# A mixture-of-experts layer on one core: in each slot the down projection of three chunks back is issued ahead of the gate and up projections

## The chip, the core and the metric

The kernel runs on one core of one Trainium2 chip. The metric is the device time of one execution in microseconds (us). The engines are PE (TensorE, the matmuls; PEld is its weight load), DVE (VectorE), ACT (ScalarE), POOL (GpSimd) and SP (SyncE, which here issues most of the DMAs). Each works through its own instructions in program order; semaphores tie them together.

## The reference

`x` is 2 x 2048 tokens of width 128. The layer is a macaron: half a feed-forward, attention with 16 heads of width 8, and half a feed-forward again with the same weights.

```python
x = x + 0.5 * ffn(layernorm(x))
x = x + attn(layernorm(x))
x = x + 0.5 * ffn(layernorm(x))
...
# ffn: 8 routed experts (top 2 of a softmax), I = 176, and one shared expert with a sigmoid gate
g = einsum('th,ehi->eti', x, w_gate)
u = einsum('th,ehi->eti', x, w_up)
eo = einsum('eti,eih->eth', silu(g) * u, w_down)
out = einsum('te,eth->th', combine, eo) + sg * (silu(x @ sw_gate) * (x @ sw_up) @ sw_down)
```

## The kernel before

All 8 experts and the shared one are computed for every token. Their 9 x 176 = 1584 hidden rows are put one after the other and cut into CH = 13 chunks of 128 (the last, the tail, has 48). Tokens come in NB = 8 blocks of 512. A step of the work is one chunk of one block, so a feed-forward has N = 104 chunks. The function `expert_phase` runs it; it is called twice, as "e1" before the attention and as "e3" after it.

For chunk n the work passes through the engines like this:

1. PE, gate (L598): three matmuls of 512 columns (high and low parts of weights and tokens) into one of two PSUM banks.
2. PE, up (L606): three matmuls into another bank. The tail chunk has no such matmuls, because its 48 up rows ride in the unused rows of its gate matmuls.
3. ACT, silu of the gate (L644).
4. POOL, times the expert's weight for each token, `cw` (L674).
5. DVE, `multiply` (L688): times up, back into PSUM.
6. ACT, `high` (L651): the product rounded to fp32r, into one of three buffers (`q_head` by name, whose room it borrows).
7. DVE, `low` (L694): what the rounding left over. It raises the semaphore `hidden_ready`.
8. PE, down (L616): three matmuls that add the chunk to the block's sum in bank Y.

PE's order is written out by hand in slots: slot s issues gate and up of chunk s and, DOWN_AFTER = 3 slots behind, the down projection of chunk s-3. DVE's order in slot s is `multiply(s)`, then `low(s-1)`; ACT's is silu of s, then `high(s-1)`. At the end of a block ACT copies bank Y out (L664), PE transposes it (L634) and DVE adds it to x (L707).

What PE waits for: gate of chunk n for the silu of chunk n-2 (for the multiply, where n-2 is a tail); up of chunk n for `low` of chunk n-4 in e1 (UPS = 4 banks), and of chunk n-3 in e3 (UPS = 3); down of chunk n for `low` of chunk n.

In e3 the object `beside` (class `Late`) puts work of the second half of the batch at the end of the slots: on PE the spreading of softmax sums (L1383), the output projection (L1398), transposes and router scores; on DVE additions and statistics (L1405, L1408), normalisation (L1443), and the router's many small steps (L1519 to L1549, slots 37 to 43).

Of the kernel before, what the change touches and what calls it, by code (L numbers as in the profile page):

```python
# [542 lines left out]
def expert_phase(nc, sem, tag, ps, x, xnT, wgate, wup, wdown, comb_rows, comb_stored, ident, room, stats=None,  # L543
# [19 lines left out]
    CW, HIDDENS, DOWN_AFTER = 8, BUFS, 3  # L563
# [12 lines left out]
    with ExitStack() as tmp:  # L576
# [11 lines left out]
        N = NB * CH  # L588

        @block.tensor  # L590
        def _(pe):
            def up(n):
                blk, c = divmod(n, CH)
                cols, tokens = slice(c * P, (c + 1) * P), slice(blk * BLK, (blk + 1) * BLK)
                if n >= 2:
                    pe.wait_ge(product if (n - 2) % CH == CH - 1 else silued, n - 1)
                for m, (wp, xp) in enumerate(PASSES):
                    last = pe.matmul(ps[:, GATE + n % 2, :], wgate[wp][:, cols], xnT[xp][:, tokens],  # L598
                                     start=(m == 0), stop=(m == len(PASSES) - 1))
                last.then_inc(gated, 1)  # L600
                if c == CH - 1:
                    return
                if n >= UPS:
                    pe.wait_ge(hidden_ready, n - UPS + 1)
                for m, (wp, xp) in enumerate(PASSES):
                    last = pe.matmul(ps[:, UP + n % UPS, :], wup[wp][:, cols], xnT[xp][:, tokens],  # L606
                                     start=(m == 0), stop=(m == len(PASSES) - 1))
                last.then_inc(upped, 1)

            def down(n):  # L610
                blk, c = divmod(n, CH)
                pe.wait_ge(hidden_ready, n + 1)
                if c == 0:
                    pe.wait_ge(summed_kept, blk + PRIME)
                for m, (wp, hp) in enumerate(PASSES):
                    last = pe.matmul(ps[:, Y, :], wdown[wp][0:rows[c], c, :], hidden[hp][n % HIDDENS][0:rows[c], :],  # L616
                                     start=(c == 0 and m == 0), stop=(c == CH - 1 and m == len(PASSES) - 1))
                last.then_inc(downed, 1)

            for s in range(N + DOWN_AFTER + 1):  # L620
                if s < N:
                    up(s)
                if DOWN_AFTER <= s < N + DOWN_AFTER:
                    down(s - DOWN_AFTER)
                if beside is not None:
                    beside.beside_pe(pe, s, SIDE)
                blk, c = divmod(s - DOWN_AFTER - 1, CH)
                if c == CH - 1 and blk >= 0:
                    pe.wait_ge(summed_kept, blk + 1 + PRIME)
                    pe.wait_ge(added, blk + PRIME)  # L630
                    if beside is not None:
                        beside.leave_bank(pe, blk)
                    for j in range(TPB):
                        tr = pe.transpose(ps[:, YT, j * P:(j + 1) * P], yT[:, j * P:(j + 1) * P], ident[:])  # L634
                    tr.then_inc(turned, 1)
# [1104 lines left out]
```

## Time and profile before

| | |
|---|---|
| median of 3 runs | 1910.42 us (1904.67 to 1911.61) |
| profiled execution, its own time | 1911.37 us |
| its span | 1909.6 us |
| mean granted PE clock over the span | 0.952 |
| PE busy | 1790.2 us, 94% |
| DVE busy | 1614.8 us, 85% |
| ACT busy | 1454.9 us, 76% |
| POOL busy | 344.6 us, 18% |
| e1, first gate matmul to the last block's addition | 67.85 to 295.87 us |
| e3, the same | 1649.90 to 1906.84 us |

Matmuls are pipelined: one of 512 columns is shown as 0.39 us long, while the next starts 0.23 us after it. So the start times of PE's rows tell its pace, and not their durations.

### The profile page before, as it was taken

The page shows a single profiled execution, that of the slowest core. Times are in us where ns is not written, and L with a number is a line of the kernel's source. Part 1 is how long each engine was busy: PE and PEld are TensorE (multiplying, and loading weights), DVE is VectorE, ACT ScalarE, POOL GpSimd, SP SyncE. Part 2 cuts the span into 40 slices and gives each one's busy share as a digit, 9 for nine tenths or more (in the row PEclk, how much of TensorE's full clock was granted, in tenths as well). Part 3 has the DMA queues.
Part 4 walks back from the last instruction along what each step waited for, and adds up shares of the span by engine and source line. Part 5 has one row for each costly group of instructions (what it writes and reads, how often), then busy time and mean ns, then how long its engine had stood idle before and what let it go on. Part 6 is the DMA issues. An engine that isn't in the chain of part 4 may idle for free. (4 is left out here: it accounts for less than half of the span.)

```text
span 1909.6 us, 37688 instructions
## 1 busy us (share of the span) xinstructions
PE 1790.2 (94%) x14923; PEld 753.7 (39%) x14923; DVE 1614.8 (85%) x1934; ACT 1454.9 (76%) x2709; POOL 344.6 (18%) x416
## 2 busy tenths in 40 slices
PE   5699996859999999999999999999999999899998
PEld 3577784701222222222222222222222223377776
DVE  6566665679999999999999999999999993377765
ACT  3455553705999999999999999999999996556454
POOL 4266660310000000000000000000000000145564
PEclk9899996857999999999999999999999998899999
DMA  4444320220000001001001001000000100433552
GB/s 116 97 122 124 120 88 1 91 92 1 20 31 27 20 26 32 20 22 36 20 20 36 22 20 33 25 20 28 30 20 25 33 28 3 87 107 113 109 135 72
DMA packets 66309, 98.81 MB, mean 52 GB/s; under 512 B 11995, under 2 KB 33312, under 8 KB 66116
## 3 DMA queue, kind: packets, MB, share of 16 engines
q1 hardware_dynamic: 61974, 94.32, 17.5%
q10 hardware_dynamic: 4160, 2.10, 0.4%
q8 instruction: 117, 1.92, 0.4%
q14 instruction: 58, 0.48, 0.1%
HBM read 84.94 MB, written 11.04 MB: 50 GB/s over the span
## 5 line engine op out<-in xcount | busy, mean ns | idle before, releaser
L1289 DVE TENSOR_REDUCE at_mx<-ps 128x1 f32<-128x1024 f32 x1024 | 1165.7, 1212 | 9.3 <-PE ps L1201 7.4
L1156 ACT ACTIVATE at_prob<-ps 128x512 f32<-128x512 f32 x2048 | 1098.0, 595 | 76.9 <-PE ps L1219 32.1
L1229 PE MATMUL ps<-at_prob,vals 128*32 128x256 f32 x8192 | 657.1, 393 | 13.2 <-ACT at_sums L1163 13.2
L1201 PE MATMUL ps<-k_head,q_head 48*128 48x512 bf16 x2048 | 638.6, 392 | 22.0 <-PEq L788 15.1
L1219 PE MATMUL ps<-q_head,k_head 51*128 51x512 bf16 x1924 | 584.3, 383 | 2.8 <-ACT at_prob L1156 2.8
L1229 PEld LDWEIGHTS ps<-at_prob,vals 128*32 128x32 f32 x8192 | 162.4, 108 | 429.2 <-ACT at_prob L1156 408.9
L674 POOL TENSOR_TENSOR e_part<-e_silu,e_cw 128x512 f32<-128x512 f32 (+1 forms) x208 | 268.2, 1290 | 301.1 <-DMA e_cw<-comb_rows 118.2
L688 DVE TENSOR_TENSOR ps<-e_part,ps 128x512 f32<-128x512 f32 (+1 forms) x208 | 144.8, 696 | 165.8 <-POOL e_part L674 165.4
L1219 PEld LDWEIGHTS ps<-q_head,k_head 51*128 51x128 bf16 x1924 | 117.6, 93 | 404.1 <-ACT at_prob L1156 384.9
L644 ACT ACTIVATE e_silu<-ps 128x512 f32<-128x512 f32 (+1 forms) x208 | 124.4, 598 | 157.7 <-PE ps L598 156.8
L651 ACT ACTIVATE q_head<-ps 128x512 fp32r<-128x512 f32 (+1 forms) x208 | 124.2, 597 | 48.8 <-DVE ps L688 38.4
L1083 POOL TENSOR_TENSOR at_mparts<-at_neg,at_zero 128x16 bf16<-128x16 f32 x32 | 7.1, 222 | 796.1 <-DVE at_neg L1303 796.1
L1201 PEld LDWEIGHTS ps<-k_head,q_head 48*128 48x128 bf16 x2048 | 119.9, 94 | 63.0 <-DVE at_mx L1289 44.8
L694 DVE TENSOR_TENSOR q_head<-ps,q_head 128x512 fp32r<-128x512 f32 (+1 forms) x208 | 142.0, 683 | 0.6
L616 PE MATMUL ps<-q_head,wdown_hi 128*128 128x512 f32 (+1 forms) x416 | 133.9, 403 | 7.1 <-DVE q_head L694 7.1
L598 PE MATMUL ps<-xnT_hi,wgate_hi 128*128 128x512 f32 x208 | 87.4, 420 | 6.7 <-PEq L1058 4.7
L616 PEld LDWEIGHTS ps<-q_head,wdown_hi 128*128 128x128 f32 (+1 forms) x416 | 78.1, 192 | 30.9 <-DVE q_head L694 9.6
L606 PE MATMUL ps<-xnT_hi,wup_hi 128*128 128x512 f32 x192 | 77.9, 406 | 9.9 <-DVE q_head L694 9.9
L616 PE MATMUL ps<-q_head,wdown_lo 128*128 128x512 f32 (+1 forms) x208 | 82.6, 397 | 0.0
L598 PE MATMUL ps<-xnT_lo,wgate_hi 128*128 128x512 f32 x208 | 82.1, 395 | 0.0
L598 PE MATMUL ps<-xnT_hi,wgate_lo 128*128 128x512 f32 x208 | 82.0, 394 | 0.0
L606 PE MATMUL ps<-xnT_lo,wup_hi 128*128 128x512 f32 x192 | 76.1, 396 | 0.0
(229 smaller groups left out, 1110.2 us busy)
## 6 DMA issues: line engine op xcount, KB each, us to landing
e_cw<-comb_rows SPq DMA_DIRECT2D x80, 256.0 KB, 3.2
e_cw<-comb_rows SPq DMA_DIRECT2D x32, 224.0 KB, 3.0
e_cw<-comb_rows SPq DMA_DIRECT2D x32, 192.0 KB, 3.0
q_head<-q_rows SPq DMA_DIRECT2D x64, 96.0 KB
k_head<-k_rows SPq DMA_DIRECT2D x64, 96.0 KB
e_cw<-comb_rows SPq DMA_DIRECT2D x32, 160.0 KB, 2.8
e_cw<-comb_rows SPq DMA_DIRECT2D x48, 96.0 KB, 2.6
e_cw<-comb_rows SPq DMA_DIRECT2D x32, 128.0 KB, 3.0
```

What stands on the lines that cost most here:

```text
L598: last = pe.matmul(ps[:, GATE + n % 2, :], wgate[wp][:, cols], xnT[xp][:, tokens], start=(m == 0), stop=(m == len(PASSES) - 1))
L606: last = pe.matmul(ps[:, UP + n % UPS, :], wup[wp][:, cols], xnT[xp][:, tokens], start=(m == 0), stop=(m == len(PASSES) - 1))
L616: last = pe.matmul(ps[:, Y, :], wdown[wp][0:rows[c], c, :], hidden[hp][n % HIDDENS][0:rows[c], :], start=(c == 0 and m == 0), stop=(c == C ...
L644: act.activation(silu[0:r, n % 2, :], ps[0:r, GATE + n % 2, :], ACT.Silu).then_inc(silued, 1)
L674: pool.tensor_tensor(part[0:r, n % 2, :], silu[0:r, n % 2, :], cw[0:r, n % CW, :], ALU.mult).then_inc(weighted, 1)
L688: dve.tensor_tensor(ps[0:rows[c], UP + n % UPS, :], part[0:rows[c], n % 2, :], up, ALU.mult).then_inc(product, 1)
L694: dve.tensor_tensor(hidden[LO][n % HIDDENS][0:r, :], ps[0:r, UP + n % UPS, :], hidden[HI][n % HIDDENS][0:r, :].bitcast(F32), ALU.subtract) ...
L1156: act.activation(prob[:, g % PROBS, c, :], ps[:, S + bank(i, g, c, last), :], ACT.Exp).then_inc(exped, 1)
L1201: one = pe.matmul(ps[:, at, :], q[i][HALF:HALF + KR, (j // CHUNKS) * P:(j // CHUNKS + 1) * P], k[i][HALF:HALF + KR, c * BLK:(c + 1) * BLK] ...
L1219: pe.matmul(ps[:, S + bank(i, g, c, last), :], k[i][0:KS, g * P:(g + 1) * P], q[i][0:KS, c * BLK:(c + 1) * BLK], start=True, stop=True).th ...
L1229: done_one = pe.matmul(ps[32 * j:32 * j + 32, O, half * HALF_BLK:(half + 1) * HALF_BLK], vals[i][:, g, :], prob[:, g % PROBS, 2 * half + j ...
L1289: dve.tensor_reduce(mx[i][:, j // 2, j % 2:j % 2 + 1], ps[:, at:at + 2, :].rearrange("p a t -> p (a t)"), AX.X, ALU.max).then_inc(max_redu ...
```

## The change

In each slot the call of `down` stands ahead of the call of `up` (which issues the gate matmuls and the up matmuls). Nothing else is touched; the counts that are waited for are the same.

```diff
             for s in range(N + DOWN_AFTER + 1):
+                if DOWN_AFTER <= s < N + DOWN_AFTER:
+                    down(s - DOWN_AFTER)
                 if s < N:
                     up(s)
-                if DOWN_AFTER <= s < N + DOWN_AFTER:
-                    down(s - DOWN_AFTER)
                 if beside is not None:
                     beside.beside_pe(pe, s, SIDE)
                 blk, c = divmod(s - DOWN_AFTER - 1, CH)
```

PE's order in e1, slot 93 (two slots into the eighth block), before the change: gate and up of chunk 93, down of chunk 90. `wgate`, `wup` and `wdown` in a name tell which it is.

```order
L598 MATMUL ps<-xnT_hi,wgate_hi 128x512 [waits e1_silued]
L598 MATMUL ps<-xnT_lo,wgate_hi 128x512
L598 MATMUL ps<-xnT_hi,wgate_lo 128x512
L606 MATMUL ps<-xnT_hi,wup_hi 128x512 [waits e1_hidden_ready]
L606 MATMUL ps<-xnT_lo,wup_hi 128x512
L606 MATMUL ps<-xnT_hi,wup_lo 128x512
L616 MATMUL ps<-q_head,wdown_hi 128x512 [waits e1_hidden_ready]
L616 MATMUL ps<-q_head,wdown_hi 128x512
L616 MATMUL ps<-q_head,wdown_lo 128x512
```

The same slot of e1 on PE after the change:

```order
L616 MATMUL ps<-q_head,wdown_hi 128x512 [waits e1_hidden_ready]
L616 MATMUL ps<-q_head,wdown_hi 128x512
L616 MATMUL ps<-q_head,wdown_lo 128x512
L598 MATMUL ps<-xnT_hi,wgate_hi 128x512 [waits e1_silued]
L598 MATMUL ps<-xnT_lo,wgate_hi 128x512
L598 MATMUL ps<-xnT_hi,wgate_lo 128x512
L606 MATMUL ps<-xnT_hi,wup_hi 128x512 [waits e1_hidden_ready]
L606 MATMUL ps<-xnT_lo,wup_hi 128x512
L606 MATMUL ps<-xnT_hi,wup_lo 128x512
```

The three down matmuls, with their wait for `hidden_ready`, moved from behind the slot's gate and up matmuls to ahead of them: six matmuls earlier. The program has as many PE rows as before, and the order of the other engines did not move.

## Rows read from the trace of the kernel before

**Rows 1.** The page: span, and busy time of engines.

```profile
span 1909.6 us, 37688 instructions
PE 1790.2 (94%) x14923; PEld 753.7 (39%) x14923; DVE 1614.8 (85%) x1934; ACT 1454.9 (76%) x2709; POOL 344.6 (18%) x416
```

**Rows 2.** Windows: length, busy us (count) of PE, PEld, DVE, ACT, POOL, PEclk, DMA, GB/s.

```profile
100.00:250.00 150.00, 149.68 (x654) 119.04 (x653) 100.38 (x173) 87.25 (x150) 91.61 (x72) 1.00 0.40 120
1680.00:1690.00 10.00, 10.00 (x44) 7.57 (x44) 7.52 (x18) 3.85 (x7) 3.87 (x3) 1.00 0.25 79
1760.00:1770.00 10.00, 7.47 (x31) 4.73 (x29) 8.16 (x16) 4.13 (x9) 5.21 (x4) 1.00 0.28 87
```

**Rows 3.** Waits in e3 (1660:1909): us in total, times, longest.

```profile
ACT e_silu L644 <- PE ps L598: 80.6, 83, 3.0
...
ACT q_head L651 <- DVE ps L688: 24.4, 19, 4.5
...
PE ps L606 <- DVE q_head L694: 8.9, 7, 3.6
```

**Rows 4.** Timeline of e1, two steady slots: start, length, engine, line.

```profile
274.00 0.39 PE L598 MATMUL ps<-xnT_hi,wgate_lo 128*128 128x512 f32 x1
...
274.43 0.60 ACT L644 ACTIVATE e_silu<-ps 128x512 f32<-128x512 f32 x1 [0.78 <-PE ps L598]
...
275.11 1.29 POOL L674 TENSOR_TENSOR e_part<-e_silu,e_cw 128x512 f32<-128x512 f32 x1 [0.75 <-ACT e_silu L644]
...
276.43 0.70 DVE L688 TENSOR_TENSOR ps<-e_part,ps 128x512 f32<-128x512 f32 x1 [0.55 <-POOL e_part L674]
...
276.95 0.61 PE L616 MATMUL ps<-q_head,wdown_hi 128*128 128x512 f32 x2
277.04 0.68 DVE L694 TENSOR_TENSOR q_head<-ps,q_head 128x512 fp32r<-128x512 f32 x1
...
277.40 0.39 PE L616 MATMUL ps<-q_head,wdown_lo 128*128 128x512 f32 x1
...
278.99 0.61 PE L616 MATMUL ps<-q_head,wdown_hi 128*128 128x512 f32 x2
```

**Rows 5.** Timeline of e1's end, from the last gate matmul (chunk 103).

```profile
286.25 0.39 PE L598 MATMUL ps<-xnT_hi,wgate_lo 128*128 128x512 f32 x1
...
287.24 0.68 DVE L694 TENSOR_TENSOR q_head<-ps,q_head 128x512 fp32r<-128x512 f32 x1
...
287.97 0.30 PEld L616 LDWEIGHTS ps<-q_head,wdown_hi 128*128 128x128 f32 x2 [1.08 <-DVE q_head L694]
287.98 0.73 PE L616 MATMUL ps<-q_head,wdown_hi 128*128 128x512 f32 x2 [0.66 <-DVE q_head L694]
...
288.54 0.40 PE L616 MATMUL ps<-q_head,wdown_lo 128*128 128x512 f32 x1
...
290.12 1.22 PE L616 MATMUL ps<-q_head,wdown_hi 128*128 128x512 f32 x2 [1.18 <-DVE q_head L694]
```

**Rows 6.** Timeline of e1's start: the first down projection.

```profile
77.03 0.73 PE L616 MATMUL ps<-q_head,wdown_hi 128*128 128x512 f32 x2 [3.46 <-DVE q_head L694]
```

**Rows 7.** Timeline of e3: down projections of chunks 11 and 102.

```profile
1695.58 0.62 PE L616 MATMUL ps<-q_head,wdown_hi 128*128 128x512 f32 x2
...
1901.09 1.21 PE L616 MATMUL ps<-q_head,wdown_hi 128*128 128x512 f32 x2 [1.17 <-DVE q_head L694]
```

**Rows 8.** Timeline of DVE in e3: side work, and multiply of chunks 40 and 44.

```profile
1735.93 2.21 DVE L1443 TENSOR_SCALAR at_oT<-x,at_small 128x128 f32<-128x128 f32 x4
...
1761.50 0.69 DVE L688 TENSOR_TENSOR ps<-e_part,ps 128x512 f32<-128x512 f32 x1 [1.52 <-POOL e_part L674]
...
1774.62 0.68 DVE L688 TENSOR_TENSOR ps<-e_part,ps 128x512 f32<-128x512 f32 x1
```

**Rows 9.** Timeline of PE in e3, a stretch at the lower clock.

```profile
1669.30 0.63 PE L598 MATMUL ps<-xnT_hi,wgate_hi 128*128 128x512 f32 x1
1669.73 0.63 PE L598 MATMUL ps<-xnT_lo,wgate_hi 128*128 128x512 f32 x1
```

## The prediction

> **What bounds the kernel now.** I read the engines' busy time first: PE is busy 94% of the span, more than any other engine [rows 1]. That is an average, so I went on to the two stages that the change touches. In the windows view, e1's middle has PE busy 149.68 of 150 us at full clock, while DVE, ACT and POOL are at 58 to 67% [rows 2]. The waits agree: in e3 the largest is ACT waiting for PE's gate (80.6 us), and PE itself waits for hidden rows 8.9 us in all [rows 3]. So the expert phases are bound by PE's stream of matmuls, and the other four steps of a chunk hide behind it. The change keeps all matmuls; what it can alter is whether they still hide.
>
> So I measured how late the hidden rows are. In the timeline of a steady part of e1 [rows 4], the last gate matmul of a chunk, call it m, starts at 274.00. Its silu starts at 274.43, POOL at 275.11, DVE's multiply at 276.43. DVE then does `low`, not of chunk m but of m-1, because its order is multiply(s), low(s-1): from 277.04 to 277.72. Where PE really waited for a `low`, at e1's end, it went on 287.98 - (287.24 + 0.68) = 0.06 us after it [rows 5]. So the down projection of chunk m-1 can start 277.72 + 0.06 - 274.00 = **3.78 us** after the last gate matmul of chunk m. It did start at 278.99, which is 1.21 us later than it could: that is the slack now.
>
> That m-1 waits for m is the point of this case. It would be easy to count only the chunk's own five steps and find much slack.
>
> **What the change does to that slack.** PE's pace: two down groups, one slot apart, start at 276.95 and 278.99, so a slot of 9 matmuls is 2.04 us and one matmul 0.227 us [rows 4]. Before, between the last gate matmul of m and down(m-1) PE has up, down, gate, up, down, gate, up: 21 matmuls, and the 22nd is the down: 22 x 0.227 = 4.99 us, as the rows show. After, the order is down(m-3), gate(m), up(m), down(m-2), gate(m+1), up(m+1), down(m-1): 12 matmuls lie between, so 13 x 0.227 = 2.95 us. Both ends moved: down(m-1) is six matmuls earlier, and down(m-3) no longer stands between. Needed are 3.78, offered 2.95: PE comes 0.83 us early and waits.
>
> Everything behind the waiting down stands still, above all the next gate, and so the wait comes back. From the start of down(m-3) to the last gate matmul of m are five matmul steps, 1.13 us; then 3.78 us to down(m-1). A **loop of 4.91 us for two slots**, where PE's work is 4.08. Two such chains, of odd and of even chunks, are interleaved and have the same period.
>
> A stalled group costs a little more: where PE waited for `low`, the third down matmul started 288.54 - 287.98 = 0.56 us behind the first [rows 5], against 277.40 - 276.95 = 0.45 without a wait [rows 4]. The weight load started only when the wait ended (287.97, after 1.08 us of idle). I take 0.10 for it: 5.01 us for two slots, **2.50 us a slot**.
>
> The Trainium skill ("TensorE: Matmul & The Clock Gate", Part 2, step 1) says that PE pulls weight loads ahead of matmuls in flight. If that went past a semaphore wait, the 0.10 would fall away; the row at 287.97 shows that it does not. By the rule the loop would be 4.91 and the time some 10 us less.
>
> *e1.* The first down starts at 77.03, released by `low` of chunk 0, which waits for the first loads of `cw` and for nothing that moved; it stays [rows 6]. The down of chunk 102 starts at 290.12 [rows 5]: 213.1 us for 102 slots. After: 102 x 2.50 = 255.0. At each tail chunk the path is a little longer, since `low` behind a 48-row multiply starts later: the last gate to down(102) is 290.12 - 286.25 = 3.87 us, 0.09 more [rows 5]; 8 of them give 0.7, with roundings 0.8. **e1: 255.8 - 213.1 = +42.7 us.** This direct look at a real wait also confirms 3.78. The block's transposes, Y copy, addition and statistics fall into the new idle time: the gap on DVE between `low` and the next multiply is 2.50 - 1.29 = 1.21 us, and they are shorter. At no cost, then; were the gap gone, they would be paid in full.
>
> *e3.* The same loop, but side work in the slots already slows it, and what is slow anyway isn't slowed again. Up to slot 14 PE is full with side matmuls (busy 10.00 of 10 in 1680:1690 [rows 2]), so there I put no loss; down(11) merely stands six matmuls earlier in its slot, 1.36 us. From down(11) at 1695.58 to down(102) at 1901.09 are 91 slots in 205.5 us [rows 7]. Of these, the four from multiply(40) at 1761.50 to multiply(44) at 1774.62 are bound by the router's steps on DVE: 13.1 us, 3.3 a slot, above 2.50 [rows 8]; they stay. The other 87 cost 87 x 2.50 = 217.5. Single pieces of DVE side work are longer than the gap of 1.21, such as the normalisation of 2.21 us, 1.0 over [rows 8]; before, slack took much of that, now there is none. There are five or six, with over 0.3 to 1.7 us each, of which the odd and even chains share some: 3 us in all, my estimate, bounds 0 and 6. Tails 0.8. **e3: 13.1 + 217.5 + 3 + 0.8 - 205.5 - 1.4 = +27.5 us.**
>
> Nothing is put down for the phase ends: down(103) follows down(102) as before. SP's loads of `cw` run eight chunks ahead and only get more time. The attention is untouched.
>
> **Sum.** 42.7 + 27.5 = +70.2 on the profiled execution's own 1911.37 gives 1981.6; the median of the runs is 1 us lower, so 1981. Bounds: without the restart and the hits, 2.45 a slot: e1 249.9 - 213.1 = 36.8, e3 13.1 + 213.2 - 205.5 - 1.4 = 19.4, together 56: 1967. With 3.87 for every path, (1.23 + 3.87) / 2 = 2.55: e1 260.1 + 0.8 - 213.1 = 47.8; e3 13.1 + 221.9 + 6 + 0.8 - 205.5 - 1.4 = 34.9; together 83: 1994. I take the middle value because the 3.78 comes from a steady stretch, 3.87 only from tails.
>
> **Rivals.**
>
> *The clock falls too (8 in 100).* PE now idles 0.4 us or so in each slot. If the granted clock went down to the lower of its two levels, 1.2 GHz, in part of the slots, a matmul step would be 1669.73 - 1669.30 = 0.43 us [rows 9] and a slot 9 x 0.43 = 3.87. For a fifth of the 208 slots that is 42 x (3.87 - 2.50) = 57 us more, 2038; for all of them some 2260. Against it: in 1760:1770 PE is busy only 7.47 of 10 us with stalls in each slot, and the clock is 1.00 [rows 2]; the new steady state is busier, (2.04 + 0.16) / 2.50 = 88% as this view counts. The same page of the Trainium skill ("A second HAM failure mode: psum-queue depth-cycling") says that short idles between groups of matmuls can make the clock swing between both levels; that is this rival, and the trace does not agree in its nearest place.
>
> *e3 hides it all (6 in 100).* If PE's and DVE's side work filled every slot of e3, only e1 would pay: 1910 + 43 = 1953. Against it: after slot 48 there is hardly any side work, and half of e3 runs like e1.
>
> *Nothing changes (3 in 100).* If `low` of a chunk waited for its own gate alone, a whole slot more would be there, 2.95 + 2.04 = 4.99 against about 4, PE would not wait, and the time be 1910. Only a different order on DVE would give that, and [rows 4] show `low` right behind the next multiply.
>
> *Faster (1 in 100).* The down projection frees the three hidden buffers. Were ACT's `high` held up by them, an earlier down would release it earlier, PE's waits of 8.9 us at the up projection in e3 [rows 3] would go, and the time be 1902. It decides if `high` waits for PE; the waits show it behind DVE's multiply alone (24.4 us [rows 3]).
>
> **How the numbers follow.** The forecast has 82 in 100, its own range 1967 to 1994. To hold 8 in 10 with some room for the loop's length, which I know to 0.1 us and which counts about 95 times in all (2 x 95 slots), I take 1960 to 2005; both the clock rival and the 1953 lie outside. A measurement of this kernel tells a change from none at about 0.5%, some 9.5 us. Faster 0.01, same 0.03, slower 0.96.
>
> **What the profile after should show.** PE waits for `q_head` L694 at the down projection (L616) in nearly every slot, about 0.3 us by this view's count, some 60 us in all; no such wait at L606 in e3. Down groups 5.0 us apart for two slots in e1, PE busy near 88% there, clock still 1.00. e1 ends near 338 instead of 295.9. The path of 3.78 us itself stays. Wrong would be: a loop of another length because POOL or DVE fall into a different order of arrival; a clock below 1; or pieces of side work in e3 that add up to far more than 3 us.

## The result: 4.75% slower

The changed kernel takes 2000.06 us (median of 4 runs, 1995.63 to 2001.45) against 1909.78 us for the kernel before (1904.67 to 1911.61): a ratio of 1.0475, 95% interval 1.0458 to 1.0491. The forecast was slower, 1981 us within 1960 to 2005. Direction and mechanism held; the loss was 90 us and not 70, and the missing 20 us are what the experiments had to find. 2000 us also lies outside the bounds that the sum itself gave, 1967 to 1994; only the range widened beyond them holds it.

The page of the changed kernel: span, busy times, and two groups of instructions with busy time, mean and the idle time before them.

```profile
span 1999.6 us, 37688 instructions
PE 1832.2 (92%) x14923; PEld 745.9 (37%) x14923; DVE 1612.5 (81%) x1934; ACT 1440.1 (72%) x2709; POOL 343.7 (17%) x416
...
L674 POOL TENSOR_TENSOR e_part<-e_silu,e_cw 128x512 f32<-128x512 f32 (+1 forms) x208 | 267.3, 1286 | 393.0 <-ACT e_silu L644 272.5
...
L616 PE MATMUL ps<-q_head,wdown_hi 128*128 128x512 f32 (+1 forms) x416 | 151.3, 445 | 68.8 <-DVE q_head L694 51.6
```

DVE, ACT and POOL do the same work in nearly the same time as in [rows 1] (ACT 14.8 us less); the span is 90.0 us longer. The down projection (L616) now has 68.8 us of idle time ahead of it, 51.6 of them for `low` (L694). "Busy" of PE rose although it does the same matmuls, since each end of a burst shows the full 0.39 us of its last matmul.

The windows of the changed kernel, e1's middle and e3's second half (columns as in [rows 2]):

```profile
100.00:300.00 200.00, 178.01 (x699) 122.70 (x698) 108.09 (x184) 86.64 (x161) 98.99 (x78) 1.00 0.31 97
1850.00:1950.00 100.00, 89.19 (x351) 61.69 (x351) 51.60 (x81) 42.69 (x80) 49.78 (x39) 1.00 0.45 117
```

PE is busy 89% in both, where it was at 99.8% in [rows 2]; the weight loads, which don't overlap each other, fell from 79% (119.04 of 150) to 61%. The clock stayed at 1.00, its upper level.

The waits of the changed kernel, first in e1 (60:345), then in e3 (1690:2000): total us, times, longest.

```profile
PE ps L616 <- DVE q_head L694: 26.6, 70, 4.8
...
PE ps L616 <- ACT e_yT L664: 7.4, 7, 1.1
```

```profile
PE ps L616 <- DVE q_head L694: 25.0, 58, 2.7
...
PE ps L616 <- ACT e_yT L664: 8.4, 7, 2.0
```

The wait at the up projection of [rows 3] is gone from e3. The wait for `low` at the down is the forecast one: 128 waits and 51.6 us in all, where the prediction expected one in nearly every slot and some 60 us. The second line of each is new and was not forecast: PE waits for the copy of the Y bank (L664), once at each of seven block ends in each phase.

### The profile page after: what moved, and what is told of

It is laid out like the page before. It is cut to its first block and busy times, and to the rows that moved or that the text cites. A ratio compares the mean times of both kernels' runs of the same rounds, so it can differ in the third digit from the quotient of the medians.

```text
span 1999.6 us, 37688 instructions
## 1 busy us (share of the span) xinstructions
PE 1832.2 (92%) x14923; PEld 745.9 (37%) x14923; DVE 1612.5 (81%) x1934; ACT 1440.1 (72%) x2709; POOL 343.7 (17%) x416
## 5 line engine op out<-in xcount | busy, mean ns | idle before, releaser
L616 PE MATMUL ps<-q_head,wdown_hi 128*128 128x512 f32 (+1 forms) x416 | 151.3, 445 | 68.8 <-DVE q_head L694 51.6
L694 DVE TENSOR_TENSOR q_head<-ps,q_head 128x512 fp32r<-128x512 f32 (+1 forms) x208 | 141.9, 683 | 0.7 <-ACT q_head L651 0.2
L616 PEld LDWEIGHTS ps<-q_head,wdown_hi 128*128 128x128 f32 (+1 forms) x416 | 63.8, 190 | 143.7 <-DVE q_head L694 137.8
L616 PE MATMUL ps<-q_head,wdown_lo 128*128 128x512 f32 (+1 forms) x208 | 82.6, 397 | 0.0
L606 PE MATMUL ps<-xnT_hi,wup_lo 128*128 128x512 f32 x192 | 75.9, 395 | 0.0
```

Of the source, the lines that this page charges most:

```text
L694: dve.tensor_tensor(hidden[LO][n % HIDDENS][0:r, :], ps[0:r, UP + n % UPS, :], hidden[HI][n % HIDDENS][0:r, :].bitcast(F32), ALU.subtract) ...
```

## Two pieces of the timeline

First, a steady part of e1 in the changed kernel, PE's rows and one weight load:

```profile
162.14 0.30 PEld L616 LDWEIGHTS ps<-q_head,wdown_hi 128*128 128x128 f32 x2 [0.61 <-DVE q_head L694]
162.14 0.72 PE L616 MATMUL ps<-q_head,wdown_hi 128*128 128x512 f32 x2 [0.19 <-DVE q_head L694]
162.70 0.40 PE L616 MATMUL ps<-q_head,wdown_lo 128*128 128x512 f32 x1
...
163.40 0.39 PE L598 MATMUL ps<-xnT_hi,wgate_lo 128*128 128x512 f32 x1
...
164.65 0.73 PE L616 MATMUL ps<-q_head,wdown_hi 128*128 128x512 f32 x2 [0.16 <-DVE q_head L694]
...
167.17 0.73 PE L616 MATMUL ps<-q_head,wdown_hi 128*128 128x512 f32 x2 [0.18 <-DVE q_head L694]
```

and DVE's of the same time:

```profile
165.83 0.70 DVE L688 TENSOR_TENSOR ps<-e_part,ps 128x512 f32<-128x512 f32 x1 [1.23 <-POOL e_part L674]
166.43 0.68 DVE L694 TENSOR_TENSOR q_head<-ps,q_head 128x512 fp32r<-128x512 f32 x1
```

Two slots last 167.17 - 162.14 = 5.03 us (forecast 5.01). From the down to the last gate matmul behind it are 163.40 - 162.14 = 1.26 us (forecast 1.13 + 0.10), and from there to the next but one down 167.17 - 163.40 = 3.77 us (forecast 3.78). DVE's multiply waits for POOL, `low` follows it, and PE goes on 167.17 - (166.43 + 0.68) = 0.06 us later. That is the loop, piece by piece.

Second, the end of the second block, where something else holds the down:

```profile
143.46 0.73 PE L616 MATMUL ps<-q_head,wdown_hi 48*128 48x512 f32 x2
...
144.91 0.40 PE L598 MATMUL ps<-xnT_hi,wgate_lo 128*128 128x512 f32 x1
...
145.34 0.60 ACT L644 ACTIVATE e_silu<-ps 128x512 f32<-128x512 f32 x1 [1.47 <-PE ps L598]
...
145.38 0.68 DVE L694 TENSOR_TENSOR q_head<-ps,q_head 128x512 fp32r<-128x512 f32 x1
...
145.84 0.59 ACT L651 ACTIVATE q_head<-ps 128x512 fp32r<-128x512 f32 x1
...
146.32 0.60 ACT L664 ACTIVATE e_yT<-ps 128x512 f32<-128x512 f32 x1
147.06 0.70 PE L616 MATMUL ps<-q_head,wdown_hi 128*128 128x512 f32 x2 [1.06 <-ACT e_yT L664]
```

The tail's down starts at 143.46 and is soon done, but ACT copies the Y bank only behind silu and `high` of that slot. The silu waits for the slot's gate, which now stands behind the down, and `high` stands behind the silu. The next block's first down overwrites Y and must wait for the copy: it starts 147.06 - 143.46 = 3.60 us after the tail's, and not 2.51. Not all of this is the copy's. The `low` that this down also waits for ends at 145.38 + 0.68 = 146.06, so without the copy the down could start at 146.12. **The copy holds it for 0.94 us, and 14 times that is 13 us.** The other 0.15 us is the longer path behind a tail, for which the prediction had 0.09.

## The experiments

The theory (A): nearly all of the 90 us are the loop through DVE plus these 14 waits. The rivals (B) differ by experiment: that the rest lies elsewhere, that the copy is only a label, or that the order of matmuls costs PE something by itself. Each ratio is against runs of the kernel before on the same chip.

| kernel | median us | ratio, 95% interval |
|---|---|---|
| e1_only | 1959.24 | 1.0275 (1.0250 to 1.0299) |
| e3_only | 1946.23 | 1.0208 (1.0186 to 1.0231) |
| after_y_first | 1986.93 | 1.0410 (1.0388 to 1.0432) |
| after_low_first | 1927.88 | 1.0106 (1.0089 to 1.0124) |
| after_low_y_first | 1912.93 | 1.0022 (1.0009 to 1.0035) |
| before_low_first | 1904.22 | 0.9980 (0.9966 to 0.9994) |
| between | 1910.57 | 1.0002 (0.9991 to 1.0014) |
| one_gate | 1979.45 | 1.0366 (1.0349 to 1.0384) |
| two_gates | 1960.18 | 1.0268 (1.0243 to 1.0293) |

The kernel before ran at 1908.48 beside the first four, 1908.30 beside the next three, 1909.30 beside the last two.

**e1_only and e3_only**: the change in one phase.

```diff
-                if DOWN_AFTER <= s < N + DOWN_AFTER:
+                if beside is None and DOWN_AFTER <= s < N + DOWN_AFTER:
                     down(s - DOWN_AFTER)
                 if s < N:
                     up(s)
+                if not (beside is None) and DOWN_AFTER <= s < N + DOWN_AFTER:
+                    down(s - DOWN_AFTER)
```

(for e3_only the two conditions are exchanged)

> The change in e1 alone; e3 keeps the order of before. Theory A (the loop of the prediction, 5.0 us for two slots, plus 1.1 us at each of 7 copies of the Y bank): the loss of e1 as the trace of after shows it, some 53 us, so 1963 us. Theory B (the prediction's sum for e1 is right, and the 19 us that it missed lie in e3): 1910 + 43 = 1953 us.

> The change in e3 alone. Theory A: 1910 + 38 = 1948 us. Theory B: the rest of the loss, 1910 + 47 = 1957 us.

Measured: e1 alone +50.8 us, e3 alone +37.8 us; together 88.6, the whole loss within the scatter of the medians. Against the prediction's 42.7 and 27.5 that is 8 and 10 us more. So the missing time lies in both phases and not in e3 alone, as B had it. That fits the seven copies in each phase (7.4 and 8.4 us in the waits above), but two totals can't show how much of it is theirs; the next run can.

**after_y_first**: ACT copies Y at the head of its slot.

```diff
+                blk, c = divmod(s - DOWN_AFTER, CH)
+                if c == CH - 1 and blk >= 0:
+                    act.wait_ge(downed, (blk + 1) * CH)
+                    act.activation(yT[:], ps[:, Y, :], ACT.Copy).then_inc(summed_kept, 1)
                 if s < N:
                     gate(s)
...
                 if 1 <= s < N + 1:
                     high(s - 1)
-                blk, c = divmod(s - DOWN_AFTER, CH)
-                if c == CH - 1 and blk >= 0:
-                    act.wait_ge(downed, (blk + 1) * CH)
-                    act.activation(yT[:], ps[:, Y, :], ACT.Copy).then_inc(summed_kept, 1)
```

> As after, but ACT copies the Y bank (L664) at the head of its slot, ahead of that slot's silu, where it stood behind silu and high. Theory A (in after, down of the first chunk of a block waits for this copy, 14 times, 15.9 us in all, on top of the loop): 2000 - 15 = 1985 us, and the wait for e_yT gone. Theory B (the label is only the last of two waits, and the loop through DVE would hold the down back just as long): 1998 to 2000 us.

Measured 1986.93 us; as ratios 1.0475 against 1.0410, about 12 us less. The idle time ahead of the down projection in its trace, PE and PEld taken together (in the changed kernel this view has 189.4 us for `low` and 15.9 for the copy):

```profile
  DVE q_head L694: 178.1, 283
  issue: 1.9, 3
```

No wait for the copy is left, so it was a real wait and most of its 15.9 us came back, not all. The traces of e1 agree with 0.94 us for each copy: from the second block's first down to the eighth's, a block takes 33.76 us in the changed kernel and 32.87 here, 0.89 less.

**after_low_first**: DVE does `low` of the last chunk ahead of `multiply` of this one.

```diff
-                if s < N:
-                    multiply(s)
                 if 1 <= s < N + 1:
                     low(s - 1)
+                if s < N:
+                    multiply(s)
```

> As after, but DVE does low(s-1) ahead of multiply(s). Theory A (low of a chunk is late only because it stands behind the multiply of the next one): low can then end 2.4 us after the last gate matmul instead of 3.7, less than the 2.95 us that PE's order offers, the loop is gone and only the waits for the Y copy stay, 14 x 1.4 = 20 us: 1930 us. Theory B (the down ahead of the gate costs by itself, by weight loads or banks): no less than 1970 us.

Measured 1927.88 us: four fifths of the loss gone with two calls exchanged on DVE, and PE's order left as in the changed kernel. Its timeline in e1:

```profile
168.26 0.40 PE L598 MATMUL ps<-xnT_hi,wgate_lo 128*128 128x512 f32 x1
...
169.18 0.62 PE L616 MATMUL ps<-q_head,wdown_hi 128*128 128x512 f32 x2
169.19 0.59 ACT L651 ACTIVATE q_head<-ps 128x512 fp32r<-128x512 f32 x1
...
169.81 0.69 DVE L694 TENSOR_TENSOR q_head<-ps,q_head 128x512 fp32r<-128x512 f32 x1 [0.35 <-ACT q_head L651]
...
170.70 0.70 DVE L688 TENSOR_TENSOR ps<-e_part,ps 128x512 f32<-128x512 f32 x1 [0.20 <-POOL e_part L674]
```

`low` now ends at 170.50, 2.24 us after the last gate matmul at 168.26, where it took 3.7. The 2.95 us that PE's order offers are enough, and PE keeps its old pace of 2.04 us a slot (its next down groups start at 171.22 and 173.26). So in steady slots the down ahead of the gate costs PE nothing by itself.

**after_low_y_first**: both edits.

> As after, with both: DVE does low(s-1) ahead of multiply(s), and ACT copies the Y bank at the head of its slot. Theory A: neither the loop nor the copy holds PE up; 1900 to 1912 us, within 0.5% of before or a little faster, since e3's old waits for low at the up projection (some 9 us) go too. Theory B (the order on PE costs by itself): over 1930 us.

Measured 1912.93 us, 0.22% above before: the copy's 15 us came back here too. It is just above what was expected, and slower than the next kernel, from which it differs in PE's order and the place of the copy. From first gate to last down group its e1 is 3.2 us longer than the next one's and its e3 5.7. In each phase 2.0 of that fall on the last twelve slots: there the gate of the last chunk stands behind one more down group, which no longer fills the wait for the last `low`. Another 1.2 are e1's first two slots (6.9 us against 5.7). The other 3.6 fall on e3's blocks with side work, and why is not shown.

**before_low_first**: DVE's edit alone, on the kernel before.

> As before, but DVE does low(s-1) ahead of multiply(s). Theory A: e1 has 1.2 us of slack and gains nothing, e3's 9 to 12 us of waits for low go: 1900 us. Theory B (those waits come from DVE's side work itself, whatever stands first): 1910 us.

Measured 1904.22 us, ratio 0.9980 with an interval that ends at 0.9994: a gain of some 4 us, less than the 8 to 10 expected. In its trace e1 is 1.8 us shorter too, from the first gate to the last down, where A expected nothing. The waits of e3 in its trace (1640:1909):

```profile
PE ps L606 <- DVE q_head L694: 4.2, 3, 2.5
PE ps L1383 <- DVE at_inv L1377: 2.3, 1, 2.3
```

The wait at the up projection more than halved: over the same stretch the kernel before has 9.9 us of it (8.9 in the shorter one of [rows 3]). I read what is left as DVE's side work, whose order did not change; part of it shows up at PE's own side matmuls. It is the fastest kernel of the study, by little.

**between**: the down stands behind the slot's gate, but still ahead of the up.

```diff
                 last.then_inc(gated, 1)
+                if DOWN_AFTER <= n:
+                    down(n - DOWN_AFTER)
                 if c == CH - 1:
                     return
...
                 if s < N:
                     up(s)
-                if DOWN_AFTER <= s < N + DOWN_AFTER:
+                elif s < N + DOWN_AFTER:
                     down(s - DOWN_AFTER)
```

> As before, but the down projection stands between the gate and the up matmuls of its slot: still ahead of the up, no longer ahead of the gate. Theory A (what counts are the matmuls between the last gate of chunk m and down of chunk m-1: 18 here, so the 19th starts after 4.3 us, more than the 3.78 needed): 1908 to 1914 us, no change. Theory B (any earlier down costs in proportion, three of six matmuls): some 1950 us.

Measured 1910.57 us, ratio 1.0002: half of the move, none of the cost.

**one_gate and two_gates**: the down stands inside the gate's group, behind its first or its second matmul.

```diff
                 for m, (wp, xp) in enumerate(PASSES):
+                    if m == 2 and DOWN_AFTER <= n:
+                        down(n - DOWN_AFTER)
                     last = pe.matmul(ps[:, GATE + n % 2, :], wgate[wp][:, cols], xnT[xp][:, tokens],
```

(`m == 1` for one_gate; the slot loop is the one of the run between)

> The down projection stands behind the first of its slot's three gate matmuls, ahead of the other two and of the up. Theory A (a loop: start of a down to the last gate matmul behind it, four steps here instead of five, then 3.78 us): (4 x 0.227 + 0.10 + 3.78) / 2 = 2.40 us a slot in place of 2.51 in after; with some 189 slots bound by it 22 us less than after, and 2 us less at the Y copies: 1976 us. Theory B (the loss is in proportion to how many of the six matmuls the down was moved ahead of, five here): 1910 + 5/6 x 90 = 1985 us.

> The down projection stands behind the second of the three gate matmuls, ahead of the third. Theory A: (3 x 0.227 + 0.10 + 3.78) / 2 = 2.28 us a slot, 43 us less than after, and 3 to 4 us less at the Y copies: 1954 us. The last gate matmul alone then carries the other 45 us, since with the down behind it there was no loss at all. Theory B (in proportion, four of six): 1970 us; and behind the third 1955 us, where 1910 was measured.

Measured 1979.45 and 1960.18 us. one_gate's down groups in e1:

```profile
160.80 0.73 PE L618 MATMUL ps<-q_head,wdown_hi 128*128 128x512 f32 x2 [0.23 <-DVE q_head L696]
...
165.60 0.73 PE L618 MATMUL ps<-q_head,wdown_hi 128*128 128x512 f32 x2 [0.22 <-DVE q_head L696]
```

4.80 us for two slots, where the loop gives 2 x 2.40. In e1 of two_gates the down groups at 114.95 and 119.53 are two slots apart: 4.58 us, where the loop gives 2 x 2.28. As whole kernels both came out above theory A: one_gate by 3 us, two_gates by 6 (1954 expected, and 10 us under B's 1970). So A has the steady slots right, and its sum for the rest is some us short. By where the down stands, behind 0, 1, 2 or 3 gate matmuls, the kernel takes 2000, 1979, 1960 and 1911 us. The first two steps give 20 us each, the third 50. In proportion to the six matmuls of the whole move it would have been 15 each. Only the last gate matmul releases the silu. Once it is ahead of its slot's down, a down holds back not the down two slots later but the one three slots later. From the start of that down to the last gate matmul are then eight matmul steps, 1.82 us; with the 3.78 that makes an estimated 5.60 us for three slots, less than the 6.12 that PE's own work takes, so nothing waits. One_gate alone hardly tells the theories apart; two_gates lies nearer to A, and between decides.

## Why the prediction was right, and where it was short

- **The bound and the slack**: right. PE was full in e1 and in most of e3, and the slack was set by `low` standing behind the next chunk's multiply. after_low_first takes away just that and the loop is gone.
- **The loop**: right. 5.01 forecast, 5.03 us measured. The 0.01 us a slot over about 189 slots is some 2 us.
- **e1, 42.7 us forecast, 50.8 measured; e3, 27.5 forecast, 37.8 measured**: short in both. The step that failed is "The block's transposes, Y copy, addition and statistics fall into the new idle time ... At no cost". For the transposes and the addition it holds: behind the block end shown above the next down groups start at 149.58 and 152.07, 2.5 us apart. For the Y copy it does not. The prediction asked whether there was idle time (it named DVE's gap, while the copy runs on ACT), not who waits for the copy and how early. In the new order the tail's down is followed by one gate and up and then by the down that needs the bank again, and the copy stands on ACT behind a silu that depends on that same gate. This term of the sum was put at 0. It measured 15.9 us of idle time, of which 13 are the copy's own by the rows above; taking it away gave 12 us on top of the loop and, with the loop gone, 15 to 16 us (1.0106 - 1.0022 of 1908). With 13 the sum would have been 1994.
- **The last 6 us**: 2 are the loop's 0.01 us a slot. 2 are e1's first two slots, put at 2.50 us each, which took 4.01 and 2.91: the first and half of the second ran at the lower clock (the rows are in the last section). The rest is about what e3's side work took above its 3 us.
- **The restart of 0.10 us**: right (162.70 - 162.14 = 0.56 us to the third down matmul, as in [rows 5]). In the changed kernel too the weight load starts only when the wait ends, at 162.14 with its matmul and after 0.61 us of idle. The Trainium skill ("TensorE: Matmul & The Clock Gate", Part 2, step 1) says that PE pulls weight loads ahead of matmuls in flight; neither trace shows it go past a wait.
- **e3's side work, 3 us with bounds 0 and 6**: from down(11) at 1747.99 to down(102) at 1992.51 the changed kernel takes 244.5 us, where the terms gave 13.1 + 217.5 + 3 + 0.8 = 234.4. Of the 10.1 above, seven copies are 6.6 and the pace of 2.51 is 1. So the 3 was low by some 2, inside its bounds.
- **The rivals**: the clock rival did not come; with PE idle for a moment in each slot for 200 us, the granted clock was 1.00. e3 did not hide its part (e3_only). No change and faster are out.
- **The signs**: PE busy 89% (88 forecast) and the clock at 1.00 came as said. e1's last addition ends at 348.1 us and not near 338, the sign that the sum for e1 was short.

That 2000 fell inside the stated range owes something to its widening: the missed term and the rest used up all of the sum's own bound and 6 us more. What stays open is small: 3.6 us of the 8.9 by which the phases of after_low_y_first and before_low_first differ, and the 3 and 6 us by which one_gate and two_gates exceed their sums.

## What to carry to other kernels

Where engines pass work round in a fixed order, don't count only a chunk's own steps: look at what stands ahead of each step on its engine, and whether the instruction you delay is what releases the one that delays it. Then a shortfall of 0.83 us is not paid once but in every turn (0.47 us in every slot here), and the cost jumps when the releasing instruction (here the last gate matmul) changes sides. For each buffer that is emptied once per block, ask not only whether the emptying engine has time but what it has queued ahead and how soon the buffer is wanted again.

## What the runs showed of the hardware

A PE that stalls about 0.2 us by this profile's count, every 2.5 us, kept its granted clock at 1.00 for 200 us (89% busy as the windows count it). The longer idle of 4.75 us ahead of the first down of e1 was followed by matmuls at the lower level, until 83.10, as these rows of the changed kernel show; the last one is from e1's end:

```profile
77.38 1.22 PE L616 MATMUL ps<-q_head,wdown_hi 128*128 128x512 f32 x2 [4.75 <-DVE q_head L694]
78.40 0.63 PE L616 MATMUL ps<-q_head,wdown_lo 128*128 128x512 f32 x1
78.83 0.63 PE L598 MATMUL ps<-xnT_hi,wgate_hi 128*128 128x512 f32 x1
...
343.71 0.73 PE L616 MATMUL ps<-q_head,wdown_hi 128*128 128x512 f32 x2 [1.73 <-DVE q_head L694]
```

Those at 78.40 and 78.83 start 0.43 us apart, 1.2 GHz in place of 2.4. The kernel before has such a stretch at the same place: 3.46 us of idle ahead of 77.03 [rows 6], then matmuls at the upper level, and from 78.61 to 81.60 some 0.43 us apart. So this drop is not the change's, though it lasts longer in the changed kernel. The length of an idle alone did not decide it: at e1's end the down behind 1.73 us of idle ran at the upper level (0.73 us), while in the kernel before the one behind 1.18 us ran at the lower (1.22 us [rows 5]). The regular short stalls cost only themselves.
